# Deformable convolution and mixture of experts: taps sampled before they are projected, row-wise hats for images 2 and 3, image 2 ahead of image 1

## What is computed

```python
def _dcn_v2(x, w_off, b_off, w_dcn):
    om = conv3x3(x, w_off) + b_off          # 18 offsets and 9 masks for each pixel
    offset, mask = om[:, :18], sigmoid(om[:, 18:])
    ys, xs = pixel + tap + offset           # fractional places, 9 for each pixel
    sampled = _bilinear_sample(x, ys, xs)   # zero outside the image
    return einsum('bckhw,ock->bohw', sampled * mask, w)

x = x + _dcn_v2(_ln_c(x), w_off, b_off, w_dcn)      # _ln_c: over the 64 channels
t = tokens(x)                                       # 1024 pixels, 64 channels
t = t + moe(_ln_t(t))      # gate, top 2 of 8, softmax, gelu(t @ W1[e] + b1) @ W2[e] + b2
```

## Time and profile before

| | us |
|---|---|
| median of 3 runs | 97.18 |
| lowest, highest | 96.42, 97.77 |
| span of the profiled execution, first to last instruction | 95.2 |
| median less span, what lies around it | 1.98 |
| PE busy in the span | 85.9 (90%) |
| DVE, ACT, POOL busy | 67.5, 45.1, 22.9 |
| bytes moved by DMA | 10.02 MB |

### The profile page before, as it was taken

How to read it: one execution, slowest core, us unless ns; L and a number is a source line. 1 busy time by engine, 2 the same in 40 slices (tenths; PEclk the granted TensorE clock), 3 DMA queues, 4 the chain that set the end, 5 groups by cost and what they waited for, 6 DMA issues and landing times.

```text
span 95.2 us, 1718 instructions
## 1 busy us (share of the span) xinstructions
PE 85.9 (90%) x574; PEld 46.9 (49%) x574; DVE 67.5 (71%) x185; ACT 45.1 (47%) x88; POOL 22.9 (24%) x33
## 2 busy tenths in 40 slices
PE   3986899899888998989999899999899999999980
PEld 3973356559545974556463544344342332223550
DVE  5695999898899997895955965957936820069550
ACT  5113575969050632341275765418462769652200
POOL 5204000000000072997200002002553150005630
DMA  1719600000419999983999994000000000000003
GB/s 47 213 30 284 267 0 3 0 7 0 121 36 274 262 253 260 260 271 112 249 257 253 251 260 123 0 0 0 3 7 0 0 0 0 0 0 0 0 7 103
DMA packets 5303, 10.02 MB, mean 105 GB/s; under 512 B 1344, under 2 KB 2400, under 8 KB 5296
## 3 DMA queue, kind: packets, MB, share of 16 engines
q1 hardware_dynamic: 4960, 9.54, 37.5%
q0 software_dynamic: 192, 0.30, 1.0%
q10 hardware_dynamic: 144, 0.10, 0.3%
HBM read 9.08 MB, written 0.85 MB: 104 GB/s over the span
## 4 chain that ended last, share of the span: by engine, by line
PE 34%; DMA 21%; DVE 17%; issue 14%; POOL 6%; SPq 3%; POOLq 1%; ACT 1%; DVEq 0%; ACTq 0%
DMA spread_hats<-hat_rows 10%; DMA hat_rows<-hrow_last 8%; PE taps_ps L791 6%; PE bank_o L882 6%; PE hid_ps L869 6%; POOL rs L326 4%; PE bank_o L817 3%; PE taps_ps L869 3%; DMA xt<-in_x_tok 2%; PE bank_c L760 2%; DVE xn L619 2%; PE bank_y L882 2%; SPq L312 2%; DVE a_sb L547 2%; DVE at L535 2%
## 5 line engine op out<-in xcount | busy, mean ns | idle before, releaser
L817 PE MATMUL bank_o<-a_sb,v_sb 128*64 128x256 f32 x144 | 18.0, 386 | 1.0 <-ACT a_sb L412 0.5
L454 ACT ACTIVATE hid<-hid_ps,b_col 128x512 f32<-128x512 f32 x18 | 11.5, 683 | 10.2 <-PE hid_ps L869 10.1
L817 PEld LDWEIGHTS bank_o<-a_sb,v_sb 128*64 128x64 f32 x144 | 9.7, 136 | 8.3 <-issue 2.3
L547 DVE TENSOR_TENSOR a_sb<-spread_hats 128x1536 f32<-128x1536 f32 x6 | 10.9, 1834 | 2.9 <-DMA spread_hats<-hat_rows 2.9
L791 PE MATMUL taps_ps<-ident,at 128*128 128x128 f32 x72 | 11.0, 280 | 1.5 <-DVE a_sb L669 0.8
L326 POOL TENSOR_TENSOR rs<-ve,power 128x2 f32<-128x2 f32 (+1 forms) x6 | 4.8, 806 | 25.7 <-DVE ve L562 21.5
L412 ACT ACTIVATE a_sb<-taps_ps 128x512 f32<-128x512 f32 x11 | 6.4, 597 | 9.2 <-PE taps_ps L791 9.2
L869 PE MATMUL hid_ps<-x2s,w_sb 64*128 64x512 f32 x36 | 10.2, 641 | 0.0
L791 PEld LDWEIGHTS taps_ps<-ident,at 128*128 128x128 f32 x72 | 7.9, 141 | 4.6 <-DVE a_sb L669 3.3
L882 PE MATMUL bank_o<-hid,w_sb 128*64 128x512 f32 x40 | 9.7, 605 | 0.0
L454 ACT ACTIVATE hid<-taps_ps,b_col 128x512 f32<-128x512 f32 x14 | 8.8, 686 | 1.5 <-PE taps_ps L869 1.5
(11 more groups left out here) (133 smaller groups left out, 121.3 us busy)
## 6 DMA issues: line engine op xcount, KB each, us to landing
spread_hats<-hat_rows SPq DMA_DIRECT2D x18, 384.0 KB, 8.1
w_sb<-in_w SPq DMA_DIRECT2D x2, 512.0 KB, 3.9
wdcn<-in_w_dcn SPq DMA_DIRECT2D x2, 144.0 KB, 3.0
xc<-in_x_ch SPq DMA_DIRECT2D x1, 256.0 KB, 4.5
hat_rows<-hrow SPq DMA_DIRECT2D x2, 128.0 KB
hat_rows<-hrow POOLq DMA_DIRECT2D x2, 128.0 KB, 8.1
xt<-in_x_tok SPq DMA_DIRECT2D x1, 192.0 KB, 2.4
out<-xc SPq DMA_DIRECT2D x1, 128.0 KB, 1.7
```

The costliest lines, as they stand in the source:

```text
L454: act.activation(hid[:, m % H_RING, half, c, :], two_banks(f"H{h}.{j}.{c}")[:, half * 512:(half + 1) * 512], ACT.Gelu, bias=b1_col[:, col: ...
L547: dve.tensor_tensor(a_sb[:, slot % A_RING:slot % A_RING + GROUP, :, :], spread_hats[:, 1:, k0:k0 + GROUP, :].rearrange("p s k t -> p k s t ...
L817: last = pe.matmul(bank_o[st * O:(st + 1) * O, 0:HW], v_sb[:, img, st, k, :], a_sb[:, slot % A_RING, st, :], start=(k == 0), stop=(k == TA ...
```

## The change

Rewritten are the path of images 2 and 3 up to DRAM, the order of sampling and projection, the bank table (now eight single banks and four pairs, lines 69 to 110 of the new file) and all four lists.

1. **Sample first.** `V`, `vs` and `xflat` go. `M{b}.{q}` multiplies the normalized pixels (`xn`, 64 channels) by A of two taps at a time (five chunks, the last of one tap): two taps land in the two halves of a bank. `se` saves each chunk (20 in all, 128x256), and `C` projects: ten matmuls of 128 columns for an image, against `wdcn`, now one load.
2. **Residual in channels.** `xr` adds the result to `xc` and `oT` transposes that; `ya` no longer adds `o_sb`.
3. **Row-wise hats for images 2 and 3.** Their pixels come in another order from the host. `om2` and `om3` put offsets, with the bias added, into a tile `big` that has three further rows: the pixel's row, its column and ones. `R{b}.0` and `R{b}.1` (two matmuls each) multiply it by a 0/1 matrix with more rows, `pick`, so that PSUM holds place minus coordinate for all hats in the layout of the DRAM rows at once. `ay`, `al`, `tm`, `tl` (ACT: abs and tanh) and `hr` (DVE) finish the hats. `omT`, `pos`, `dist`, `relu`, `haty`, `hT` and `hs` of these images go.
4. The constants for that: POOL makes a single-partition tile `crow` (`rows0`: five iotas and a memset), seven small DMAs of SP put its pieces into `big`, and SP issues the loads of w1, w2 and xc behind them.
5. **Spreads by two taps.** Each image has its own buffer, so the wait of L304 goes. There are 15 DMAs for an image, 12 of 256 KB and three of 128 KB, the same bytes in rows of 2 KB (1 KB in the last chunk) where they had 3 KB. `pd` writes its product in place.
6. **Orders.** Images 2 and 3 stand right behind image 0 in the front, and image 1's convolution behind theirs. `sel0` of POOL moves from behind `dw3` to behind `rstd1`.

```diff
-GROUP = 3
+CHUNKS = (TAPS + 1) // 2
-DIRECT, HAT_RING = 2, 3
+DIRECT, SPREAD = (0, 1), (2, 3)
...
-    "rstd0 rstd1 dw3 rstdt0 sel0 rstdt1 rstdt2 rstdt3 ya0.0 ya0.1 ya0.2 ya0.3 ya1.0 ya1.1 ya1.2 "
+    "rstd0 rows0 rstd1 sel0 dw3 rstdt0 rstdt1 rstdt2 rstdt3 ya0.1 ya0.2 ya0.3 ya1.1 ya1.2 "
...
+            sp.wait_ge(pool_rows, 6)
+            sp.wait_ge(pick_ready, 1)
+            for r in range(3):
+                row = slice(POS_ROW + r, POS_ROW + r + 1)
+                sp.dma_start(om_sp[row, :, :], crow[:, r * HW:(r + 1) * HW].unsqueeze(1).broadcast_to([1, len(SPREAD), HW])).then_inc(ld_pos, 16)
...
-                for g in range(UNITS):
-                    u = UNITS * b + g
-                    if i > 0:
-                        sp.wait_ge(tap_made, upto(f"pd{u - UNITS}"))
-                    taps = slice(GROUP * g, GROUP * g + GROUP)
+                for q in range(CHUNKS):
+                    taps = slice(chunk_taps(q)[0], chunk_taps(q)[-1] + 1)
                     flat = rows[i, :, :, taps, :].rearrange("c x k t -> c x (k t)")
...
+                elif kind == "R":
+                    i = SPREAD.index(b)
+                    pe.wait_ge(ld_pos, 16 * 7)
+                    pe.wait_ge(*saved(om_saved, f"om{b}"))
+                    if n[1] == 0:
+                        take_bank(step, (rows_abs, upto(f"ay{b}")))
+                        for c in range(2):
+                            last = pe.matmul(bank(step)[:, c * HW:(c + 1) * HW], pick[c], om_sp[:, i, :], start=True, stop=True)
...
+                    for st in range(ST):
+                        for place, k in enumerate(taps):
+                            col = place if len(taps) == 2 else st
+                            last = pe.matmul(bank(step)[col * C:(col + 1) * C, 0:HW], xn[:, NT * b + st, 0, :], tap(b, k, st),
+                                             start=(st == 0 or len(taps) == 1), stop=(st == ST - 1 or len(taps) == 1))
...
+                    for q in chunks:
+                        for j in range(NT):
+                            last = pe.matmul(bank(f"C{b}.0")[j * O:(j + 1) * O, 0:P], wdcn[:, q, :], smp[:, b, q, j * P:(j + 1) * P],
+                                             start=(q == 0), stop=(q == CHUNKS - 1))
```

More of the change, by code:

```diff
@@ L92 @@
-BANK = {step: home for home, steps in HOMES.items() for step in steps.split()}
-def engine_of(step):
-    return next(n for n, order in ORDERS.items() if step in order)
-def upto(step):
-    order = ORDERS[engine_of(step)]
-    kind = kind_of(step)
-    return sum(kind_of(s) == kind for s in order[:order.index(step) + 1])
+HOMES = (
+    (
+        "xnT0 conv0 omT0 conv3 R3.1 T1.7 M3.0 wdT1 O1.2 O1.3.1 "
+    ),
+    (
+        "xnT2 xnT1 conv1 T0.3 T0.4 M0.2 M1.2 M2.1 C2.0 O0.3 "
+    ),
+    (
+        "xnT3 R2.1 omT1 T0.6 T1.1 T1.4 M1.3 C1.0 oT1 xT1 M3.2 C3.0 oT3 O1.3.0 Fa1.0 "
+    ),
+    (
+        "conv2 R2.0 T0.0 T0.1 T0.8 M0.4 C0.0 oT0 M3.4 O0.1 F0 Fa1.1 "
+    ),
+    (
+        "T0.2 T0.7 M0.1 M1.0 M1.4 M2.0 xT2 O1.1 "
+    ),
+    (
+        "R3.0 T0.5 M0.0 M0.3 T1.0 T1.2 T1.8 xT3 "
+    ),
+    (
+        "T1.3 M1.1 M2.2 M2.3 M2.4 M3.1 oT2 O0.0 O1.0 "
+    ),
+    (
+        "T1.5 T1.6 xT0 M3.3 wdT0 O0.2 "
+    ),
+)
@@ L110, in kind_of @@
+PAIR_HOMES = (
+    (
+        "H0.0.0 H0.2.1 sp0.0 H1.0.1 sp1.0 H1.2.0 "
+    ),
+    (
+        "gate0 H0.1.1 H0.3.1 H1.2.1 H1.3.1 "
+    ),
+    (
+        "H0.2.0 H0.0.1 H0.3.0 gate1 H1.1.0 sp1.1 "
+    ),
+    (
+        "H0.1.0 sp0.1 H1.0.0 H1.1.1 H1.3.0 "
+    ),
+)
+BANK = {step: home for home, steps in enumerate(HOMES) for step in steps.split()}
+PAIR = {step: home for home, steps in enumerate(PAIR_HOMES) for step in steps.split()}
 def kind_of(step):
@@ L117, in numbers, with engine_of, upto, chunk_taps @@
     return [int(n) for n in step[len(kind_of(step)):].split(".")]
+def engine_of(step):
+    return next(n for n, order in ORDERS.items() if step in order)
+def upto(*steps):
+    order = ORDERS[engine_of(steps[0])]
+    last = max(order.index(step) for step in steps)
+    return sum(kind_of(s) == kind_of(steps[0]) for s in order[:last + 1])
+def chunk_taps(q):
+    return range(2 * q, min(2 * q + 2, TAPS))
 def metaformer_kernel(nc, x_tok, x_ch, w_off, b_off, w_dcn, wg, bg, w1, b1, w2, b2, out):
@@ L353, in _ @@
                     make_sel()
+                elif kind == "rows":
+                    make_rows()
                 elif kind == "rstd":
@@ L710, in _ @@
+                    dve.tensor_tensor(xc[:, b, part], home[:, part], xc[:, b, part], ALU.add).then_inc(fin_ready, 1)
         @block.tensor
         def _(pe):
-            released = {}
-            def take(name, *waits):
-                for sem_, value in released.get(name, ()):
-                    pe.wait_ge(sem_, value)
-                released[name] = waits
-            def keep_warm(n, bank):
-                for _ in range(n):
-                    pe.matmul(bank[:, 0:P], ident[:, :], ident[:, :], start=True, stop=True)
@@ L856, in _ @@
                     for q in range(2):
[L857 to L858 removed]
+                        rows_ = slice(q * SECOND, q * SECOND + 2 * E)
+                        last = pe.matmul(two_banks(step)[:, q * 512:(q + 1) * 512], sel[rows_, 2 * i + q, :], wt[rows_, h, :], start=True, stop=True)
                     last.then_inc(spread_done, 1)
```

700 lines of the change are left out of this document (351 added, 349 removed), and 28 rows, old and new, of tables (ACT_ORDER, DVE_ORDER, PE_ORDER).

## The result

The changed kernel takes 90.48 us in the median of four runs (89.73 to 94.86), against 97.17 before: 0.929 of its time, 95% interval 0.920 to 0.937. Forecast were 95.0 us and 91.8 at the lowest. The profiled execution took 90.21 us, its span is 88.4; before, the span was 95.2.

The account below looks back on a forecast made before the run. The prediction took the serial path of hats, write and spreads of images 2 and 3 as the bound, PE close behind. Span 95.2 - (72.03 - 69.9) = 93.1, plus 1.98, gave 95.1, stated as 95.0 us; range 91.8 to 99.2.

Parts of the forecast that it names:

- First spread at 21.0: SP's first spread of image 2 goes out at 21.0 us, before 26.8; bounds 20.4 and 23.
- Image 3's first spread 16.3 later: Image 3's first spread follows image 2's by 16.3 us, as before the change, so at 37.3.
- Chunk 3.1 lands 9.4 after that, at 255 GB/s: Image 3's second chunk lands 9.4 us after its first spread, at 46.7; M3.1 then runs 47.9 to 48.9.
- PE by itself would end M3.1 at 46.7: PE's own work up to M3.1's end: 45.3 us without waits, plus 1.4 for waits in the front.
- So it waits about 2.2 us: PE waits about 2.2 us for the DMA in front of M3.0 and M3.1, delaying six H behind them.
- 20.6 and 0.4 us from M3.1 to H1.0.0: PE's steps between M3.1 and H1.0.0: 20.6 us of work, 0.4 for hops; H1.0.0 starts at 69.9, before 72.03.
- the rest, 23.2: From H1.0.0 to the end: the same steps in another order, left at 23.2 us.
- PE's work does not shrink by a visible amount: All of PE's work: -9.4 us removed, +8.4 added, so -1; bounds -3 to +2.
- A write that doesn't queue: Image 3's hats land while image 2's spreads run; image 3's spreads go 2.3 us earlier, span 92.9; chance 0.18.
- A write with a fixed price: Image 3's hat write takes 7.85 us by itself; spreads start at 40.2, total 98.0, no change; chance 0.18.
- Spreads priced by the row: All 30 spreads cost 193 ns per row, not by bytes; H1.0.0 at 84.4, total 109.6; chance 0.08.
- Losses: Front or experts lose 2 to 4 us to late `rows0`, T waits or ACT's order: 97 to 99; chance 0.10.

Follow-up runs that it names:

- the last two runs: Changed kernel with unread extra H, O-like and transpose steps behind PE's last step, alternating in one, grouped by kind in the other: medians 110.31 and 109.36 us.

## Why the prediction was wrong

**Step by step.**

- *First spread at 21.0*: 20.66. The number held, the working only in part: `rows0` was at the low end, but `sel` was not on the chain. ACT's copy stood at 13.17 behind `om2` and waited for nothing; the convolutions and R on PE were the chain.
- *Image 3's first spread 16.3 later*: 16.1 later, 36.74.
- *Chunk 3.1 lands 9.4 after that, at 255 GB/s*: 8.1 after (44.81). The 255 was read from one window of the kernel before; in the new one image 2's spreads ran at 299 with 2 KB rows and at 287 with 3 KB rows.
- *PE by itself would end M3.1 at 46.7*: 47.1 less the wait of 0.7 is 46.4. Held, though through two errors: less work than I had, and 2.5 us of waits in the front where I had allowed 1.4.
- *So it waits about 2.2 us*: 0.70, and 1.24 and 1.87 in the two later profiles of the same steps. The first step that failed, with 1.8 us of the miss (M3.1 at 47.1, not 48.9); its size in this one execution is in part luck. Had the chunk come as late as forecast, the loss would probably have been more than the wait, as the clock in the runs with 4 KB rows and with image 1 ahead suggests.
- *20.6 and 0.4 us from M3.1 to H1.0.0*: 19.4; *the rest, 23.2*: 21.9. The second step that failed, "PE's work does not shrink by a visible amount", and in it the terms "six H at 0.96" (0.88), "three O at 1.87" (1.71 to 1.79) and "I leave their 23.2". The change in parts was right (-0.8 against -1); the term that was left out is the price of 38 fewer changes of kind, which measured -4.3 on the steps common to both. By the last two runs' 0.17 a change it would be 6.5, and 5.8 for the 34 fewer changes of shape, so the size fits roughly, not closely: that not every change costs the same is likely, and not measured. That the 4.3 are this price is inferred from the extra work behind the end; the one run that took groups apart in place was mixed up with waits.

1.8 + 1.6 + 1.3 is the miss of 4.7 us of span (93.1 against 88.4). That the gain was forecast at all, from the earlier spreads, is right for the wrong reason: PE's work made most of it.

**The premise.** "Images 2 and 3 set the pace through one serial path" was the smaller half of the truth for the kernel before. I took the chain that ended last for the bound, and wrote beside it that PE was nearly as long, without asking by how much. The kernel before with its DMA path 2.4 us faster gained 0.7 on PE and 1.1 in time. What the new front and the earlier spreads do is keep the path out of the way of a PE whose work is now 5 us shorter: with the write 7 us later the whole gain but 1% is gone. So the gain has two parts that need each other, 4.9 us of PE's work and 1.8 of its waits, which together are 6.7 of the 6.8 us of span.

**The rivals.** *A write that doesn't queue* gave the nearest time, 92.9, for another reason: the break between the images' spreads is still there (1 GB/s in slice 17). *A write with a fixed price* fell: 5.21 us now, 7.85 before. *Spreads priced by the row* fell the other way: shorter rows were faster. My line there that "the windows with short rows agree" was misread: 318 GB/s with 1.5 KB rows against 410 with 4 KB is 29% more time per byte, far from the 1.5% of the estimate beside it. *Losses* of 2 to 4 us did not come; PE waited 3.1 us in all behind the start, 4.9 before.

**The shape of a step.** In the profile's rows an H is 64*128 (rows by columns of the array), an O 128*64, a transpose 128*128. The Trainium skill (TensorEngine Tiling, Key Properties) says that a change of the tiling mode, not of the tile alone, drains TensorE. The trace agrees as far as it goes: O0.1 at 57.13 stands between two C, which are 128*64 as well, and took 58.84 - 57.13 = 1.71, where an O between H and transposes took 1.87. In the kernel before, four tap transposes between other steps of 128*128 took 0.44 (from 16.14), and between two M, which are 128*64, 0.56 (from 28.89). So the price goes with the shape; no run changed the kind and kept the shape, or the reverse. I had not weighed this rule at all, and it speaks about the one thing that the change did most of.

**The write and the spreads.** Image 3's last write was issued by 31.52 and had landed at 36.73, while the spreads of image 2 ended with slice 16, at 35.4. The Trainium skill (DMA: Bandwidth & Descriptors, Queues, rings and completion order) says that the increment of the semaphore lands only after every earlier write of the same DMA engine, over its queues. That would explain a write that is told only when the spreads have drained. The traces say that it is not the main part here. GpSimd's queue has 192 packets, all of them this write. Before, it was issued from 33.85 us on, and not one of its packets ran until 39.65; then all ran between the spreads' own, up to 42.5, and the write had landed at 43.10. Now its first packets ran at 31.3, 3.9 us after the first issue at 27.35, and the last at 35.6. So its own packets start late while spreads are queued, and at most the last microsecond is left for the increment. And in the run with the late write it had landed at 37.3, 5.8 us after its last issue, with image 2's spreads going on at 309 GB/s, so it does not need them drained either. Why the packets start late is open; that they then run between the spreads' packets fits the rule of turns that I had weighed.
